# Position-bias tables of an attention layer: source plane built earlier, strips loaded by two queues, inverse of the softmax sums at a later place in the loop

## The reference, cut to what matters

```python
idx = jnp.arange(H * W)
hh, ww = (idx // W, idx % W)
dist = jnp.abs(hh[:, None] - hh[None, :]) + jnp.abs(ww[:, None] - ww[None, :])
bias = spatial_bias[:, 0][dist]          # 59 values, larger distances clipped to the last
q, k, v = proj(wq, bq), proj(wk, bk), proj(wv, bv)
scores = jnp.einsum('bhqd,bhkd->bhqk', q, k) / jnp.sqrt(16.) + bias
ctx = jnp.einsum('bhqk,bhkd->bhqd', softmax(scores), v)
resid = ctx @ wo + bo + x
out = (resid - mu) * rsqrt(var + 1e-5) * ln_gamma + ln_beta
```

## Time and profile before

| what | us |
|---|---|
| median of 3 runs | 10369.0 (10361.93 to 10372.07) |
| the profiled execution, its own time | 10373.92 |
| its span, first to last instruction | 10372.1 |
| TensorE busy in it | 9606.5 (93%) |
| VectorE busy | 7181.1 (69%) |
| ScalarE busy | 5674.1 (55%) |
| GpSimd busy | 963.2 (9%) |

### The profile page before, as it was taken

The page is one execution under the profiler, slowest core; times in us unless marked ns, Lnnn a source line. Parts: engine busy times, 40 slices in busy tenths (PEclk is TensorE's granted clock), DMA queues, the critical chain, the costliest instruction groups (busy, mean ns, idle before and its releaser), DMA issues.

```text
span 10372.1 us, 345836 instructions
## 1 busy us (share of the span) xinstructions
PE 9606.5 (93%) x139471; PEld 4590.9 (44%) x139471; DVE 7181.1 (69%) x24584; ACT 5674.1 (55%) x11896; POOL 963.2 (9%) x862
## 2 busy tenths in 40 slices
PE   7888851699999999999999999999999999999998
PEld 4444430244444444444444444444444444444444
DVE  3555540577777777777777777777777777777774
ACT  1111100266666666666666666666666666666665
POOL 0222220100100010001000100011001100110001
PEclk8888875699999999999999999999999999999999
DMA  2444434100110011001100110011001100110000
GB/s 54 86 85 87 85 85 31 49 10 16 35 29 11 14 36 31 11 14 36 32 10 14 34 34 9 15 31 34 11 15 30 29 17 13 33 28 19 10 13 15
DMA packets 443040, 324.25 MB, mean 31 GB/s; under 512 B 75495, under 2 KB 436424, under 8 KB 440520
## 3 DMA queue, kind: packets, MB, share of 16 engines
q1 hardware_dynamic: 433988, 299.91, 12.5%
q10 hardware_dynamic: 7488, 2.77, 0.5%
HBM read 197.66 MB, written 104.87 MB: 29 GB/s over the span
## 4 chain that ended last, share of the span: by engine, by line
PE 75%; ACT 3%; DMA 2%; SPq 1%; issue 1%; DVE 0%; POOL 0%; ACTq 0%; POOLq 0%; DVEq 0%
PE l_ps L1006 51%; PE l_ps L1084 22%; ACT p L1187 2%; DMA sums_scratch<-ctx_raw 1%; PE l_ps L1099 1%; PE l_ps L1115 1%; ACT rows L1179 1%; PE l_ps L1116 0%; PE l_ps L1102 0%; SPq L842 0%; DMA sums<-sums_scratch 0%; PE l_ps L1096 0%; SPq L837 0%; SPq L830 0%; DMA stacks_scratch<-parts 0%
## 5 line engine op out<-in xcount | busy, mean ns | idle before, releaser
L1187 ACT ACTIVATE p<-l_ps 128x448 f32<-128x448 f32 x10976 | 5263.9, 543 | 2691.4 <-PE l_ps L1006 2683.9
L1228 DVE CUSTOM_DVE_ANT_0 summed<-l_ps,pair_bias 128x448 f16<-128x448 f32 x9408 | 5379.8, 619 | 1792.0 <-PE l_ps L1006 1776.2
L1006 PE MATMUL l_ps<-ks,qs 64*64 64x448 f16 x21952 | 3925.8, 355 | 59.3 <-DVE partial L1228 35.0
L1006 PE MATMUL l_ps<-high,id 64*64 64x448 f16 x21952 | 3928.9, 354 | 27.6 <-ACT p L1187 3.0
L1006 PE MATMUL l_ps<-qs,ks 64*64 64x448 f16 x21952 | 3922.7, 354 | 0.0
L1006 PE MATMUL l_ps<-low,id 64*64 64x448 f16 x21952 | 3902.4, 352 | 0.7 <-issue 0.7
L1006 PE MATMUL l_ps<-rows,pick_row 64*64 64x448 f16 x21952 | 3874.2, 349 | 0.0
L1084 PE MATMUL l_ps<-p,v 128*32 128x448 f32 x22400 | 2413.9, 547 | 0.0
L1006 PEld LDWEIGHTS l_ps<-high,id 64*64 64x64 f16 x21952 | 1204.1, 106 | 1493.8 <-issue 981.0
L1006 PEld LDWEIGHTS l_ps<-ks,qs 64*64 64x64 f16 x21952 | 1204.1, 106 | 877.0 <-DVE partial L1228 573.6
L1006 PEld LDWEIGHTS l_ps<-qs,ks 64*64 64x64 f16 x21952 | 1205.6, 106 | 394.0 <-issue 0.4
(11 more groups left out here) (130 smaller groups left out, 4285.7 us busy)
## 6 DMA issues: line engine op xcount, KB each, us to landing
stacks_scratch<-parts SPq DMA_DIRECT2D x448, 112.0 KB
x<-in_x SPq DMA_DIRECT2D x16, 1568.0 KB
ks<-stacks_scratch SPq DMA_DIRECT2D x32, 784.0 KB, 9.6
qs<-stacks_scratch SPq DMA_DIRECT2D x224, 112.0 KB, 2.8
recip<-inverse_scratch SPq DMA_DIRECT2D x448, 56.0 KB, 2.0
h_scratch<-x SPq DMA_DIRECT2D x8, 1568.0 KB
w_scratch<-x SPq DMA_DIRECT2D x8, 1568.0 KB
mh<-h_scratch SPq DMA_DIRECT2D x64, 196.0 KB
```

Source lines behind the costliest of these rows:

```text
L1006: last = nc.tensor.matmul(ps[h * BT:(h + 1) * BT, bank, 0:CH], lhs(part, h), rhs(part, h), start=start, stop=True, skip_group_check=not start)
L1187: nc.scalar.activation(p[unit % PB][:], ps[:, bank_of(unit), 0:CH], ACT.Exp).then_inc(exp_done, 1)
L1228: nc.vector.tensor_tensor_reduce(summed[unit % 2][:], ps[:, AB + unit % MAXIMA, 0:CH], bias.rearrange("p s t -> p (s t)"), 1.0, LOWEST, AL ...
```

## The change

- prepare_layer0 also loads the 59 bias values, a one-hot matrix for one quadrant only (56 x 56 distances, 59 x 3136) and a mirror matrix; between r = 0 and r = 1 it makes the quadrant as a line with 7 matmuls, passes it through DRAM, and at its end mirrors it with two matmuls into the 111 x 111 plane, kept in SBUF.
- layer0, at its first image, stores 8 copies of the plane, each shifted by one column (111 x 104), and then loads from them the first EARLY = 7 of 13 strips of every partition: 16 DMAs, each for 8 partitions, with rows of 3328 bytes. All of this is on SyncE's queue, between the first loads of x and the first store_branch.
- prepare_tables loads the other 6 strips (8 DMAs on each of two queues), and of the two copies into pair_bias VectorE now makes one.
- layer1 loads the first block of x ahead of the weights, waits for one cleared tile only before it loads wo, and clears the context and mask tiles after the weights have come; TensorE and ScalarE do the first transposition before they wait for weights. v0 and five tiles of p lie where the early strips were.
- the inverse is taken at i = 13 (was 9), stored at 14 (10), loaded at 15 (11), multiplied at 19 (14); I_MIX is 28 (27).

The core of the diff:

```diff
+STRIP = BW * SPAN
+EARLY = 7
...
+    far = np.minimum(np.arange(H)[:, None] + np.arange(W)[None, :], DIST - 1).reshape(-1)
+    pick = (np.arange(DIST)[:, None] == far[None, :]) * 1.0
+    mirror = (np.arange(W)[:, None] == np.abs(np.arange(DIAG) - (W - 1))[None, :]) * 1.0
...
+            sp.dma_start(dist[:], a["L1_conv_spatial_bias"][:, 0:1], allow_slow_non_contiguous=True).then_inc(dist_loaded, 16)
+            sp.dma_start(pick[:], a["dist_pick"]).then_inc(dist_loaded, 16)
+            sp.dma_start(mirror[:], a["mirror"]).then_inc(dist_loaded, 16)
+            sp.wait_ge(line_copied, H * W // FAR)
+            sp.dma_start(scr["quarter"].rearrange("h w -> (h w)").unsqueeze(0), line[:]).then_inc(line_kept, 16)
+            sp.wait_ge(line_kept, 16)
+            sp.dma_start(quarter[:], scr["quarter"]).then_inc(quarter_in, 16)
...
+                if r == 0:
+                    pe.wait_ge(dist_loaded, 48)
+                    for f in range(H * W // FAR):
+                        if f >= 3:
+                            pe.wait_ge(line_copied, f - 2)
+                        nc.tensor.matmul(ps[0:1, 4 + f % 3, 0:FAR], dist[:], pick[:, f * FAR:(f + 1) * FAR],
+                                         start=True, stop=True).then_inc(picked, 1)
+            pe.wait_ge(quarter_in, 16)
+            pe.wait_ge(line_copied, H * W // FAR)
+            nc.tensor.matmul(ps[0:W, 4, 0:DIAG], quarter[:], mirror[:], start=True, stop=True).then_inc(plane_ready, 1)
+            pe.wait_ge(plane_copied, 1)
+            nc.tensor.matmul(ps[0:DIAG, 5, 0:DIAG], half_plane[:], mirror[:], start=True, stop=True).then_inc(plane_ready, 1)
...
+                if k == 2 * NK - 1:
+                    for n in range(H * W // FAR):
+                        act.wait_ge(picked, n + 1)
+                        nc.scalar.copy(line[:, n * FAR:(n + 1) * FAR], ps[0:1, 4 + n % 3, 0:FAR]).then_inc(line_copied, 1)
+            act.wait_ge(plane_ready, 1)
+            nc.scalar.copy(half_plane[:], ps[0:W, 4, 0:DIAG]).then_inc(plane_copied, 1)
+            act.wait_ge(plane_ready, 2)
+            nc.scalar.copy(plane[:], ps[0:DIAG, 5, 0:DIAG]).then_inc(plane_copied, 1)
...
+def load_strips(eng, scr, near, half, first, count, done):
+
+    t = scr["planes"]
+    for ih in range(BW):
+        p0 = half * BT + ih * BW
+        src = bass.AP(t.tensor, t.offset + (first * BW + BW - 1 - ih) * SPAN, [[DIAG * SPAN, BW], [STRIP, count], [1, STRIP]])
+        eng.dma_start(near[p0:p0 + BW, :, 0:STRIP], src).then_inc(done, 16)
...
@@ -290,6 +334,11 @@
                 if before is None:
                     for r in range(2):
                         load_image(b, r)
+                    for iw in range(BW):
+                        sp.dma_start(scr["planes"][iw], w["plane"][:, BW - 1 - iw:BW - 1 - iw + SPAN]).then_inc(scr["planes_kept"], 16)
+                    sp.wait_ge(scr["planes_kept"], BW * 16)
+                    for half in range(2):
+                        load_strips(sp, scr, w["near"], half, 0, EARLY, scr["near_in"])
...
-        pick, dist = sb("pick", [DIST, N]), sb("dist", [DIST, 1])
-        line = sb("line", [1, N])
-        near = sb("near", [128, SPAN, SPAN])
-        ps = ctx.enter_context(nc.psum_tensor("tab_ps", [128, 8, 512], F32))
-        loaded, picked, copied, kept = sem("tab_loaded"), sem("tab_picked"), sem("tab_copied"), sem("tab_kept")
-        spread, rounded, low_done, high_done = sem("tab_spread"), sem("tab_rounded"), sem("tab_low_done"), sem("tab_high_done")
+        late = sb("late", [128, NR - EARLY, STRIP + 8])
...
-        near_rows = lambda r: near[:, r * BW:(r + 1) * BW, :].rearrange("p h (s w) -> p s h w", w=BW)
+        strip = lambda r: w["near"][:, r, 0:STRIP] if r < EARLY else late[:, r - EARLY, 0:STRIP]
+        near_rows = lambda r: strip(r).rearrange("p (h s w) -> p s h w", s=NR, w=BW)
...
-        def spread_lines(eng, ih):
-
-            t = scr["dist"]
-            for half in range(2):
-                for iw in range(BW):
-                    p0 = half * BT + ih * BW + iw
-                    src = bass.AP(t.tensor, t.offset + (BW - 1 - ih) * DIAG + BW - 1 - iw, [[1, 1], [DIAG, SPAN], [1, SPAN]])
-                    eng.dma_start(near[p0:p0 + 1, :, :], src).then_inc(spread, 16)
...
         @block.sync
         def _(sp):
-            sp.dma_start(pick[:], a["dist_pick"]).then_inc(loaded, 16)
-            sp.dma_start(dist[:], a["L1_conv_spatial_bias"][:, 0:1], allow_slow_non_contiguous=True).then_inc(loaded, 16)
-            sp.wait_ge(copied, len(pieces))
-            sp.dma_start(scr["dist"].rearrange("s j -> (s j)").unsqueeze(0), line[:]).then_inc(kept, 16)
-            sp.wait_ge(kept, 16)
-            for ih in range(0, BW, 2):
-                spread_lines(sp, ih)
-
-        @block.tensor
-        def _(pe):
-            pe.wait_ge(loaded, 32)
-            for n, (i, m) in enumerate(pieces):
-                if n >= 8:
-                    pe.wait_ge(copied, n - 7)
-                nc.tensor.matmul(ps[0:1, n % 8, 0:m], dist[:], pick[:, i:i + m], start=True, stop=True).then_inc(picked, 1)
+            load_strips(sp, scr, late, 0, EARLY, NR - EARLY, late_in)
 
         @block.scalar
         def _(act):
-            for n, (i, m) in enumerate(pieces):
-                act.wait_ge(picked, n + 1)
-                nc.scalar.copy(line[:, i:i + m], ps[0:1, n % 8, 0:m]).then_inc(copied, 1)
-            act.wait_ge(kept, 16)
-            for ih in range(1, BW, 2):
-                spread_lines(act, ih)
-            act.wait_ge(spread, 2 * BT * 16)
+            load_strips(act, scr, late, 1, EARLY, NR - EARLY, late_in_too)
+            act.wait_ge(scr["near_in"], 2 * BW * 16)
             for r in range(NR):
+                if r == EARLY:
+                    act.wait_ge(late_in, BW * 16)
+                    act.wait_ge(late_in_too, BW * 16)
                 nc.scalar.copy(block_rows(w["high"][:, r]), near_rows(r)).then_inc(rounded, 1)
 
         @block.vector
@@ -639,18 +659,15 @@
                 dve.wait_ge(rounded, r + 1)
                 nc.vector.tensor_tensor(block_rows(w["low"][:, r]), near_rows(r), block_rows(w["high"][:, r]),
                                         ALU.subtract).then_inc(low_done, 1)
-            dve.wait_ge(low_done, NR)
+                nc.vector.tensor_copy(w["pair_bias"][0:BT, r], w["high"][0:BT, r, PAIR_FROM:NR]).then_inc(low_done, 1)
+            dve.wait_ge(low_done, 2 * NR)
...
             for r in range(NR):
                 pool.wait_ge(rounded, r + 1)
-                if r:
-                    pool.wait_ge(high_done, 2 * r)
-                nc.gpsimd.tensor_copy(w["pair_bias"][0:BT, r], w["high"][0:BT, r, PAIR_FROM:NR]).then_inc(high_done, 1)
-                pool.wait_ge(high_done, 2 * r + 1)
                 nc.gpsimd.tensor_copy(w["pair_bias"][BT:2 * BT, r], w["high"][BT:2 * BT, r, PAIR_FROM - 1:NR - 1]).then_inc(high_done, 1)
-            pool.wait_ge(high_done, 2 * NR)
+            pool.wait_ge(high_done, NR)
...
+        VSIZE = KTILES * HEADS * VW + 32 - VW
+        reused = w["near"][:].rearrange("p r d -> p (r d)")
+        v = [reused[:, 0:VSIZE], sb("v1", [128, VSIZE])]
+        p = [reused[:, VSIZE + i * CH:VSIZE + (i + 1) * CH] for i in range(5)] + [sb(f"p{i}", [128, CH]) for i in range(5, PB)]
...
-        I_ROWS, I_MIX = NP - LEAD + 2, 27
+        I_ROWS, I_MIX = NP - LEAD + 2, 28
...
-            sp.wait_ge(set_up, 1)
+            load_x(0)
             for dst, src in ((wq, "L1_conv_wq"), (wk, "L1_conv_wk"), (wv, "L1_conv_wv"), (wo_all, "L1_conv_wo")):
                 load(dst[:, :], a[src])
             for dst, src in ((bq, "L1_conv_bq"), (bk, "L1_conv_bk"), (bv, "L1_conv_bv")):
@@ -898,11 +917,11 @@
             load(bo, a["L1_conv_bo"].unsqueeze(0))
             for dst, src in ((gamma, "L1_conv_ln_gamma"), (beta, "L1_conv_ln_beta")):
                 load(dst[:], a[src].partition_broadcast(128))
+            sp.wait_ge(set_up, 1)
             for g in range(NG):
                 for j in range(HG):
                     h = g * HG + j
                     load(wo[32 * j:32 * j + DK, g, :], a["L1_conv_wo"][h * DK:(h + 1) * DK, :])
-            load_x(0)
             load_x(1)
             sp.wait_ge(folded_in, 1)
...
-                if n >= 1 and i == 10:
+                if n >= 1 and i == 14:
                     store_inverse(k)
-                if n >= 1 and i == 11:
+                if n >= 1 and i == 15:
                     load_inverse(k)
...
-                if n >= 1 and i == 14:
+                if n >= 1 and i == 19:
                     divide(n - 1)
...
+            side(SIDE_X, 0)
             pe.wait_ge(loaded, LOADS * 16)
             nc.tensor.matmul(ps[0:1, CB, 0:C], bv[:], wo_all, start=True, stop=True).then_inc(set_up, 1)
             pe.wait_ge(set_up, 4)
             for m in range(NB):
-                for step in range(4):
+                for step in range(0 if m else 1, 4):
                     side(SIDE_X + step, m)
```

(44 more changed lines are left out.)

21 lines of the change are left out of this document (9 added, 12 removed).

## The result

| | before | after | predicted |
|---|---|---|---|
| median, us | 10367.56 (4 runs) | 10045.86 (10044.59 to 10047.52, 4 runs) | 10038 (10010 to 10080) |
| ratio | | 0.969, interval 0.9673 to 0.9707 | |
| span of the profiled execution | 10372.1 | 10044.2 | |

A forecast was written before the change was run, and what follows sets the result against it. It saw TensorE bounding layer 1's loop, with a 303.0 us table hole before it. 10373.9 - 266 (tables) - 13.2 (set-up) + 6.5 (preparation) + 0 (image 0) - 58.6 (inverse) = 10042.6; less 4.9 for the median, 10038 us, range 10010 to 10080.

The forecast's parts named there:

- 1. Tables: Table stage between the layers: 303 us shrink to 37 (29 to 48), a gain of 266 us (255 to 274).
- 12 to 27 us, plus some 3 to start and land: Late strips' loads in prepare_tables: 8 engines at 96 to 216 GB/s, 0 to 9 us late for round 8, 3 taken.
- The second queue: Late strips' loads in prepare_tables: a second queue saves only the issue of 8 DMAs, about 6 us, no bandwidth.
- 2. The set-up: Layer 1's set-up: SyncE starts loading at once instead of waiting for VectorE's clearing, gain 13.2 us (10 to 15).
- 4. Image 0: Layer 0's first image: added plane stores and strip loads fit SyncE's idle time, free at 173 before 188, cost 0 us.
- the rival of one engine: Layer 0's first image: plane's stores run on one engine, SyncE free at 250, 28 us lost, 10066 us; chance 0.12.
- 5. The inverse: Layer 1's loop: four slots later, the inversion stops waiting for sums at n % 14 = 0 and 12, gain 58.6 us (45 to 59).
- The sentence on I_MIX: Loop's projection at slot 28 beside a V projection at 29: up to 1 us in 7 units either way, 0 taken.
- The clock: TensorE's clock rise from 0.50 to 0.98 comes 30 us into the loop, half of that lost: 10053 us; chance 0.10.
- The waits for sums: In the loop they stay, since keys land late more often than in the trace: 10097 us; chance 0.06.
- The strips as the wait: Table stage: 3328-byte rows move no faster by byte than 416-byte ones, 102 us, stage 117, total 10118; chance 0.04.
- The projection waiting for the inverse: Loop, slot 28: TensorE waits 56 times if the inverse's chain exceeds 21.5 us, kernel slower than before; chance 0.02.

The follow-up runs named there:

- Experiment 7: Changed kernel with the late strips put together in DRAM during layer 0's first image and fetched by two DMAs over 64 partitions: 10028.51 us.
- Experiment 5: Changed kernel with all 16 loads of late strips on SyncE's queue alone: 10055.21 us.
- experiment 4: Changed kernel with layer 1's set-up in the old order (memsets, then weights, then x): 10055.72 us.
- experiment 11: Kernel before with an unused tile ahead of layer 0's tiles, so that they lie in SBUF as in the changed kernel: 10364.98 us, one run.
- experiments 1 and 2: Kernel before with only the loop's inverse moved four slots later: first with I_MIX = 28, 10317.32 us; second with I_MIX left at 27, 10308.62 us.
- experiment 3: Changed kernel with I_MIX back at 27: 10043.4 us.

## Why the prediction was right, by its own steps

**The bound.** The hole between the layers was most of the gain, 259.2 of 328 us in the span.

**1. Tables, 266 predicted, 259.2 measured.** In the sum of 37 us, two terms were off and partly cancelled. ScalarE's 8 issues took 3.5 us, not 6, and a round of VectorE's 1.7 us, not 2.07: remainders of 1.00 to 1.58 us and copies of 0.33 to 0.91, where 1.47 and 0.6 were taken. Without its wait the stage would have taken 27.6 us, not 34. But the step "12 to 27 us, plus some 3 to start and land", from which 3 us of waiting were taken, failed: the strips took 31.5 us, beyond the 15 to 30 that it allowed, against the 24 that a wait of 3 us at round 8 implies, and VectorE stood at round 8 after 16.3 us and not after 21, so that the wait was 16.2. The number of engines was right, 8; their rate was not: 75 to 92 GB/s on 8 engines, below the lower of the two bounds (96, from the loads into 56 partitions). It was taken from rows of 512 bytes and more in other DMAs, and no row showed 3328-byte rows to 8 partitions. Experiment 7 puts the cost of that pattern at 16.3 us of the stage, 3.5 of them ScalarE's issues.

**The second queue** was priced at the issue of 8 DMAs, 6 us. Experiment 5 measures 5.6 us in the stage, nearly the number, by another way: shorter landing. That the numbers meet is luck; the issue itself was worth nothing, since the strips were the wait.

**2. The set-up, 13.2 predicted.** 13.5 between the traces, 13.4 by experiment 4.

**3. The preparation, 6.5 predicted,** 6.15 measured. Line and quadrant hid as said.

**4. Image 0, 0 predicted, 0 measured,** with a term far off: 38 us for the plane's stores, when the 888 rows went by from 118.4 to 126.9, each 33 ns of an engine. The window holds a share of 0.22, 3.5 engines:

```profile
118.00:127.00 9.00, 8.03 (x72) 6.80 (x71) 3.08 (x5) 2.34 (x5) 0.00 (x0) 0.50 0.22 43
```

The 0.13 us per row were those of reads of 416-byte rows into one partition each. The divisor 3 for 111 rows was about right, and the rival of one engine (0.12) falls with it.

**Layer 0 as a whole** was said to be unchanged; it is 5.8 us shorter, most likely by the place of its tiles (experiment 11). No term had this, and 5.8 us of luck stand in the total: without them the sum would have missed by 13.7 us, not by 7.9. The 4.9 us taken off for the median were a step of their own that failed. The old table stage took 303.0 us in the profile that the sum starts from, and 300.8, 299.7 and 294.0 in the three other profiles that have it (experiments 11, 1 and 2). So the profiled execution seems to have been long in the very stage that the change takes out, the 266 us already held that excess, and the profiled execution of the changed kernel, 10046.01 us, lay at its median. The 7.9 us missed are thus 6.8 from the tables, 3.9 from the loop and 4.9 from this step, less layer 0's 5.8 and some 2 in small terms.

**5. The inverse, 58.6 predicted.** The term itself is right: 59.0 in the units it named, of which 56.0 with I_MIX left at 27 (experiment 3), and experiments 1 and 2 show that it needs no other part of the change. The sentence on I_MIX was mis-sized: "up to 1 us in 7 units either way, 0 taken", from the neighbour at slot 29. Measured: some 0.4 us gained in each unit from 8 to 13 but for 9, and 2.3 us lost in each at 9, the latter not from TensorE's neighbours but through the norm, the store behind it and the load of x behind that in SyncE's queue. The prediction went through SyncE's queue for the steps at slots 14 and 15 and not for slot 48.

**The rivals.** SyncE in image 0: free at 138, no. The clock: 0.95 in the loop's first 15 us, no. The waits for sums: gone but for 1.0 us outside the tail. The strips as the wait: the mechanism was there, in a mild form, 31.5 us and not 102. The projection waiting for the inverse: no such row in the loop.

## What to carry to other kernels

Price a DMA by the number of partitions in its outer dimension, and where a kernel needs 8 odd-shaped pieces quickly, let an earlier stage with idle queues lay them out in DRAM so that one transfer over 64 partitions can fetch them. When a step moves by a slot, follow what waits for its result on every in-order queue, to the end of the unit and into the next: here the price of one slot stood seven transfers behind a store. And when a stage that was not touched changes its length, look at where its tiles lie before counting the difference to the change.
